# Grouped attention layers on one core: one product for the softmax denominators amid the next tile, reciprocals on transposed columns

## The reference

```python
N_HEADS, N_KV_HEADS, HEAD_DIM = 16, 4, 32
def rmsnorm(x, w, eps=1e-05):
    inv = jax.lax.rsqrt(jnp.mean(x * x, axis=-1, keepdims=True) + eps)
    return x * inv * w
q = (rmsnorm(x, norm_w) @ wq).reshape(B, T, 16, 32)
k = (cond @ wk).reshape(B, S, 4, 32)
v = (cond @ wv).reshape(B, S, 4, 32)
qg = q.reshape(B, T, 4, 4, 32)
scores = jnp.einsum('btgrd,bsgd->bgrts', qg, k) / sqrt(32)
attn = softmax(scores, axis=-1)
out = jnp.einsum('bgrts,bsgd->btgrd', attn, v).reshape(B, T, 512)
x = x + out @ wo
```

## Time and profile before

| | |
|---|---|
| median of 3 runs | 4080.01 us |
| the profiled run | 4083.46 us |
| its span, first to last instruction | 4081.7 us |
| TensorE busy | 3991.6 us (98%) |
| VectorE busy | 2434.2 us (60%) |
| ScalarE busy | 2094.2 us (51%) |
| GpSimd busy | 2035.3 us (50%) |
| granted clock of TensorE, mean | 0.989 |

### The profile page before, as it was taken

How to read it: one execution, slowest core, us unless ns; L and a number is a source line. 1 busy time by engine, 2 the same in 40 slices (tenths; PEclk the granted TensorE clock), 3 DMA queues, 4 the chain that set the end, 5 groups by cost and what they waited for, 6 DMA issues and landing times. The chain is left out here.

```text
span 4081.7 us, 52317 instructions
## 1 busy us (share of the span) xinstructions
PE 3991.6 (98%) x19446; PEld 2636.9 (65%) x19446; DVE 2434.2 (60%) x3455; ACT 2094.2 (51%) x2728; POOL 2035.3 (50%) x1097
## 2 busy tenths in 40 slices
PE   9999999998999999999968999999999999999999
PEld 7888888886566666666544555555555555555555
DVE  3221210011755566556638888888888888888885
ACT  3111221121544454444527776776677677767765
POOL 0000000001655566556736777677667677776766
PEclk9999999998999999999979999999999999999999
DMA  5343522233645555555423333333333333333332
GB/s 185 129 135 133 170 96 85 79 114 91 161 125 139 136 135 134 137 135 132 116 70 88 88 89 88 100 101 100 84 100 91 90 99 98 99 89 92 100 78 67
DMA packets 312792, 447.01 MB, mean 110 GB/s; under 512 B 44728, under 2 KB 116408, under 8 KB 312552
## 3 DMA queue, kind: packets, MB, share of 16 engines
q1 hardware_dynamic: 312552, 443.84, 38.8%
HBM read 215.07 MB, written 102.77 MB: 78 GB/s over the span
## 5 line engine op out<-in xcount | busy, mean ns | idle before, releaser
L1943 DVE TENSOR_REDUCE a_max_cols<-a_ps 128x1 f32<-128x512 f32 x1536 | 1028.5, 675 | 265.5 <-PE a_ps L2077 257.2
L1826 ACT ACTIVATE a_probs<-a_ps 128x1024 f32<-128x1024 f32 x768 | 774.6, 1024 | 378.3 <-PE a_ps L2108 372.7
L2077 PE MATMUL a_ps<-a_k_ops,a_q_ops 96*128 96x512 f32 x1536 | 653.3, 427 | 24.1 <-DVE a_max_cols L1943 17.5
L1724 POOL TENSOR_TENSOR a_sums<-a_probs 128x1024 f32<-128x1024 f32 x192 | 455.3, 2391 | 336.0 <-ACT a_probs L1826 336.0
L1047 DVE TENSOR_REDUCE a_max_cols<-a_ps 128x1 f32<-128x512 f32 x512 | 340.8, 688 | 273.4 <-PE a_ps L1211 273.3
L2077 PEld LDWEIGHTS a_ps<-a_k_ops,a_q_ops 96*128 96x128 f32 x1536 | 291.8, 190 | 312.5 <-issue 141.6
L2108 PE MATMUL a_ps<-a_q_ops,a_k_ops 128*128 128x512 f32 x1536 | 486.6, 398 | 1.1 <-ACT a_probs L1826 1.1
L807 POOL MEMSET a_ident<- 128x128 f32 x1 | 0.2, 204 | 975.5 <-issue 975.5
L1724 POOL TENSOR_TENSOR a_sums<-a_sums,a_probs 128x1024 f32<-128x1024 f32 x192 | 454.4, 2389 | 0.1
L2122 PE MATMUL a_ps<-a_probs,a_v 128*32 128x512 f32 x3072 | 411.1, 607 | 0.7 <-ACT a_probs L1826 0.6
L303 DVE TENSOR_TENSOR cp_c_lo<-cp_raw,cp_c_hi 128x1024 fp32r<-128x1024 f32 x64 | 78.4, 1226 | 529.2 <-ACT cp_c_hi L247 529.1
(11 more groups left out here) (154 smaller groups left out, 7347.0 us busy)
## 6 DMA issues: line engine op xcount, KB each, us to landing
a_k_ops<-k_scratch SPq DMA_DIRECT2D x192, 256.0 KB, 4.4
a_q_ops<-a_qn_hi SPq DMA_DIRECT2D x768, 64.0 KB, 2.0
k_scratch<-cp_out SPq DMA_DIRECT2D x88, 512.0 KB, 2.8
cp_raw<-in_ctx_t SPq DMA_DIRECT2D x64, 512.0 KB, 4.1
a_q_ops<-a_qn_hi SPq DMA_DIRECT2D x256, 128.0 KB, 2.3
x_raw<-out_t SPq DMA_DIRECT2D x25, 1024.0 KB, 7.2
a_q_ops<-a_qn_lo SPq DMA_DIRECT2D x384, 64.0 KB, 2.0
a_x_res<-out_t SPq DMA_DIRECT2D x92, 256.0 KB, 3.1
```

Source lines behind the costliest of these rows:

```text
L1724: pool.tensor_tensor(sums[:, hp], (probs if n < H else sums)[:, hp], probs[:, n], ALU.add)\
L1826: act.activation(probs[:, n], ps[:, 2 * (n % 2):2 * (n % 2) + 2, :], ACT.Exp).then_inc(exped, 1)
L1943: dve.tensor_reduce(max_cols[:, t % 2, col:col + 1], bank(b), AX.X, ALU.max, negate=True)\
L2077: pe.matmul(bank(b), q_ops[0:SHIFT, s, h, q * P:(q + 1) * P], k_ops[0:SHIFT, s, :], start=True, stop=True).then_inc(smax, 1)
```

## The change

GpSimd makes all six sums of probabilities of a tile: the four of before, then, once the tile's last outputs are done, sums 6 and 7, which are written over probabilities 6 and 7. The denominators become one group of products, moved behind outputs 0 of the next tile. VectorE transposes them out of PSUM in blocks of 32 x 32, so that each query's value stands in its own row and one column of each of 16 blocks is enough; it takes the reciprocal of these 16 columns, spreads them back with a second transpose whose input repeats the column, and makes the normalisation, which GpSimd made before. ScalarE no longer copies the denominators. The mean square goes the same way (transpose, 16 columns, transpose), its product moves to maximum 3 of tile 3 and to the bank of the outputs; the last quarter of squares is added ahead of sum 4 of tile 2, and one split of x moves from tile 3 to tile 0. The diff, cut to its core:

```diff
-            def sum_squares(n):
-                for k in range(1, CK):
+            def sum_squares(n, quarters=range(1, CK)):
+                for k in quarters:
...
-                if n >= H:
-                    pool.wait_ge(summed, g * SUMS + n - H + 1)
+                wait(pool, summed, g * SUMS + max(n - H + 1, 0))
                 pool.wait_ge(exped, g * NS + n + 1)
-                pool.tensor_tensor(sums[:, hp], (probs if n < H else sums)[:, hp], probs[:, n], ALU.add)\
-                    .then_inc(summed, 1)
+                if n >= NS - H // 2:
+                    pool.wait_ge(pv, (g + 1) * KT)
+                    pool.tensor_tensor(probs[:, n], sums[:, hp], probs[:, n], ALU.add).then_inc(summed, 1)
+                else:
+                    pool.tensor_tensor(sums[:, hp], (probs if n < H else sums)[:, hp], probs[:, n], ALU.add)\
+                        .then_inc(summed, 1)
...
-            def normalise(it, t):
-                g = tile_no(it, t)
-                pool.wait_ge(recip_done, (g + 1) * PARTS)
-                pool.wait_ge(out_taken, g + 1)
-                pool.tensor_tensor(stage[:, t % 2, :], out_raw[:, :], stage[:, t % 2, :], ALU.mult).then_inc(normed, 1)
...
+                    if there(it, t - 1):
+                        sum_probs(*at(it, t - 1), 6)
+                        sum_probs(*at(it, t - 1), 7)
...
+                    if t == 2 and there(it, 2 * T):
+                        sum_squares(it + 2, range(CK - 1, CK))
                     sum_probs(it, t, 4)
                     sum_probs(it, t, 5)
-                    if there(it, t - 1):
-                        normalise(*at(it, t - 1))
                     if t == 1 and there(it, 2 * T):
-                        sum_squares(it + 2)
+                        sum_squares(it + 2, range(1, CK - 1))
...
-            def take_denominators(it, t):
-                g = tile_no(it, t)
-                act.wait_ge(den_done, g + 1)
-                wait(act, o_lo, g - 1)
-                act.activation(stage[:, t % 2, :], bank(FB), ACT.Copy).then_inc(den_taken, 1)
...
-            def reciprocal(it, t, i):
+            def turn_denominators(it, t):
                 if there(it, t):
-                    n = S // PARTS
-                    if i == 0:
-                        dve.wait_ge(den_taken, tile_no(it, t) + 1)
-                    part = stage[:, t % 2, i * n:(i + 1) * n]
-                    dve.reciprocal(part, part).then_inc(recip_done, 1)
+                    g = tile_no(it, t)
+                    dve.wait_ge(den_done, g + 1)
+                    wait(dve, recip_made, g)
+                    dve.wait_ge(ms_step, 2 * inverted(*at(it, t + 1)))
+                    dve.transpose(turned_cols(), bank(FB)).then_inc(den_turned, 1)
+
+            def reciprocal(it, t):
+                if there(it, t):
+                    g = tile_no(it, t)
+                    dve.wait_ge(den_turned, g + 1)
+                    wait(dve, recip_done, g)
+                    dve.reciprocal(recip_col[:, :, :], cols[:, :, 0:1]).then_inc(recip_made, 1)
+
+            def spread_reciprocals(it, t):
+                if there(it, t):
+                    g = tile_no(it, t)
+                    dve.wait_ge(recip_made, g + 1)
+                    wait(dve, o_lo, g - 1)
+                    dve.transpose(stage[:, t % 2, :].rearrange("p (i j) -> p i j", j=d),
+                                  recip_col[:, :, :].broadcast_to([P, S // d, d])).then_inc(recip_done, 1)
+
+            def normalise(it, t):
+                if there(it, t):
+                    g = tile_no(it, t)
+                    dve.wait_ge(recip_done, g + 1)
+                    dve.wait_ge(out_taken, g + 1)
+                    dve.tensor_tensor(stage[:, t % 2, :], out_raw[:, :], stage[:, t % 2, :], ALU.mult)\
+                        .then_inc(normed, 1)
...
-                        invert_mean_square(it + 1, 2)
-                        invert_mean_square(it + 1, 3)
+                        split_x(it + 1, 1)
                     if t == 1 and there(it, T):
                         for k in range(0 if first else 2, CK):
                             split_x(it + 1, k)
                     if t == 3 and there(it, 2 * T):
                         split_x(it + 2, 0)
-                        split_x(it + 2, 1)
                     maximum(it, t, 1)
                     maximum(it, t, 2)
                     if t == 1:
                         where(dve, it, par, 1, lambda: rest_wo(it // B))
-                    reciprocal(*at(it, t - 1), 0)
                     maximum(it, t, 3)
+                    if t == T - 1 and there(it, 2 * T):
+                        turn_squares(it + 2, OUTB)
                     maximum(it, t, 4)
-                    reciprocal(*at(it, t - 1), 1)
+                    if t == T - 1 and there(it, 2 * T):
+                        invert_mean_square(it + 2)
+                    if t == 1 and first:
+                        spread_roots(1)
                     maximum(it, t, 5)
                     if there(it, t + AHEAD):
                         take_q(*at(it, t + AHEAD))
                     maximum(it, t, 6)
                     if t == 0 and first:
-                        mean_square(1, FB)
-                    if t == T - 1 and there(it, 2 * T):
-                        mean_square(it + 2, FB)
+                        turn_squares(1, FB)
+                    turn_denominators(*at(it, t - 1))
                     maximum(it, t, 7)
                     maximum(it, t, 8)
-                    reciprocal(*at(it, t - 1), 2)
+                    if t == 0 and first:
+                        invert_mean_square(1)
+                    reciprocal(*at(it, t - 1))
                     maximum(it, t, 9)
+                    spread_reciprocals(*at(it, t - 1))
                     maximum(it, t, 10)
                     if there(it, t - LAG):
                         add_result(it, t)
                     maximum(it, t, 11)
-                    reciprocal(*at(it, t - 1), 3)
-                    if t == 0 and first:
-                        for i in range(PARTS):
-                            invert_mean_square(1, i)
+                    normalise(*at(it, t - 1))
...
-                for h in range(H):
-                    pe.matmul(ps[h * d:(h + 1) * d, FB, :], ones[:, 0:d],
-                              probs[:, LATE * (H // 2) + h // 2, h % 2, :], start=True, stop=False,
-                              skip_group_check=True)
+                if there(it, t + 1 + AHEAD):
+                    pe.wait_ge(q_taken, g + 1 + AHEAD + 1)
                 pe.wait_ge(summed, (g + 1) * SUMS)
                 for h in range(H):
-                    last = pe.matmul(ps[h * d:(h + 1) * d, FB, :], ones[:, 0:d], sums[:, h // 2, h % 2, :],
-                                     start=False, stop=True, skip_group_check=True)
+                    last = pe.matmul(ps[h * d:(h + 1) * d, FB, :], ones[:, 0:d], probs[:, NS - H // 2 + h // 2, h % 2, :],
+                                     start=True, stop=True, skip_group_check=True)
...
-                    wait(pe, den_taken, tile_no(it, t))
-                    if there(it, t + AHEAD):
-                        pe.wait_ge(q_taken, tile_no(it, t) + AHEAD + 1)
-                    if t == T - 1 and there(it, 2 * T):
-                        pe.wait_ge(ms_step, MS * (it + 2) + 1)
+                    pe.wait_ge(den_turned, tile_no(it, t))
...
-                    denominators(*at(it, t - 1))
...
+                    if t == T - 1 and there(it, 2 * T):
+                        pe.wait_ge(out_taken, tile_no(it, t))
+                        sum_squares(it + 2, OUTB)
...
-                    if t == T - 1 and there(it, 2 * T):
-                        pe.wait_ge(q_taken, tile_no(it, t) + AHEAD + 1)
-                        sum_squares(it + 2, FB)
+                    denominators(*at(it, t - 1))
```

More of the change, by code:

```diff
@@ L1452, in grouped_layers @@
     scale = d ** -0.5
[L1453 to L1456 removed]
+    SUMS = (KT - 1) * (H // 2)
+    SQ = CK + 2
     LEAD = M + 6
@@ L1856, in batch @@
                         squares(1)
-                    if t == 1 and there(it, T):
-                        act.wait_ge(q_taken, (it + 1) * T)
+                    if t == (1 if it == 0 else 0) and there(it, T):
                         inv_rms(it + 1)
@@ L2023, in batch @@
                     maximum(it, t, 15)
-            mean_square(0, OUTB)
-            for i in range(PARTS):
-                invert_mean_square(0, i)
+            turn_squares(0, OUTB)
+            invert_mean_square(0)
             rest_wq(0)
+            spread_roots(0)
             for t in range(AHEAD):
@@ L2033, in _ @@
             pairs(dve, batch)
-            for i in range(PARTS):
-                reciprocal(N - 1, T - 1, i)
+            turn_denominators(N - 1, T - 1)
+            reciprocal(N - 1, T - 1)
+            spread_reciprocals(N - 1, T - 1)
+            normalise(N - 1, T - 1)
             add_result(N, 0)
```

63 lines of the change are left out of this document (37 added, 26 removed).

## The result

The changed kernel takes 4289.89 us (median of 4 runs, 4285.07 to 4294.19) against 4080.12: a ratio of 1.0514, 95% interval 1.0496 to 1.0532. It is 210 us slower, where 17 us faster was forecast, and far above the range. The profiled execution took 4285.07 us.

What follows compares the result with a forecast made beforehand. TensorE, busy 98% of the span, was taken as the bound. -82.6 (product) + 48 (GpSimd late) + 18 (weights) = -17 us: 4066 us for the profiled run, 4063 median; own range 4030 to 4085, whole range 4002 to 4112.

Steps and rivals of the forecast that it cites:

- TensorE is the bound and one product less is worth 0.86 us a tile: In each tile on TensorE, one product of denominators fewer saves 0.86 us, 82.6 us over 96 tiles.
- VectorE's new chain: VectorE's transpose of the denominators, taken as 0.69 us, ends 0.3 us before TensorE needs the bank: free.
- rival 3: VectorE's transposes are long (1.3 us) or the SBUF one takes turns with GpSimd: 4092 to 4107 us; chance 0.14.
- GpSimd's load: GpSimd's sums, remainders and squares need 71.7 us a block against TensorE's 77.0, 93%: throughput suffices.
- rival 4: GpSimd's sums arrive later than the denominators' product in every tile, so TensorE's path is not shortened: 4080 us; chance 0.03.
- The normalisation on VectorE: Asked amid sum 4, it ends 0.54 us after that sum; GpSimd's lateness then becomes TensorE's wait at maximum 14.
- How late GpSimd is: GpSimd's lateness makes TensorE wait 0.1, 0.75, 0.1 and 1.05 us in tiles 0 to 3: 48 us over 24 blocks.
- Rival 2: In tile 2 the normalisation waits 1.9 us for all of sum 4, clock may drop: 4080 to 4117 us; chance 0.22.
- Weights: At new weights (wo three times, wq twice) VectorE's remainders alternate with GpSimd's sums: 18 us, ends 0 and 30.
- Ends of the stage: The start saves about 4 us, the end waits about 4 us for sums 6 and 7: zero, plus or minus 5.

Runs made afterwards that it cites:

- both collisions away: Changed kernel with an SBUF transpose in place of the normalisation (multiplication left out) and tile 1's two x splits ahead of maximum 0: 4056.24 us, ratio 0.9937.
- three benches: Separate kernels computing nothing of the reference: VectorE asks amid trains of three GpSimd instructions, of ten, and of ten beside TensorE, ScalarE and loads; no total time given.
- the first bench: Computes nothing of the reference: 72 groups of three GpSimd additions, VectorE asking at growing delays with two-operand instructions or a 16-column scaling; no total time given.

## Why the prediction was wrong, step by step

- *TensorE is the bound and one product less is worth 0.86 us a tile*: nearly right in size (0.78 in the mean with both collisions away, 0.87 in the best tiles), as long as nobody is next. That ScalarE's copy of the denominators was worth nothing was wrong: without the rest of the change it is what is next (0.22 us a tile).
- *VectorE's new chain*: right. Transposes took 0.72 us out of PSUM and 0.70 out of SBUF, for the 0.69 that I took; the output projection did not wait. That excludes rival 3.
- *GpSimd's load*: right. The denominators waited 6.4 us for GpSimd, all of it at the end of the stage; rival 4 fell.
- *The normalisation on VectorE*: the step that failed. It read "whoever comes second waits for the whole instruction of the other" out of the earlier trace rows and priced every collision at the rest of one instruction, 0 to 2 us. That is a lower end. In the kernel three GpSimd instructions in a row went ahead of the normalisation, until GpSimd had nothing ready: 6.05 us where the rest of the sum was 1.98. The earlier trace rows show GpSimd giving way at 1183.5 with an instruction ready; they were 30 of 30, and I took a thing seen 30 times for a rule, though nearly all of the 30 asked at one place, 1.64 us into the sum. The range had no row for the other outcome.
- The Trainium skill, "SBUF — State Buffer", section "SBUF: two separate sides", says whoever starts first holds the port pair for its whole instruction. The trace agrees on the instruction that is running (every turn ends 0.55 us behind it). It does not follow that the blocked one is next, and the 6.05 us show that it need not be.
- *How late GpSimd is*: tile 2, where I saw the normalisation slip in ahead of sum 4, is the worst: it came 0.41 us after sum 4 had begun. Tile 1's splits did not hold sum 6 up; sum 6 held the second split, for 1.94 us of TensorE's time. Tile 3, which I had at 1.05 us, lost nothing there in most blocks (0.83 us; 3.16 to 4.85 in four).
- *Rival 2* named the place, tile 2, and the fall of the clock, which is 82 of the 98 us by which the other products grew. Its price was one turn, 1.9 us; 4.72 were paid. With the one wait before sum 5, which brings the price back to one turn, the time was 4146, so its 4080 to 4117 was too low even there: the splits' 1.94 us, which I had at 0.75, stay.
- *Weights*: forecast 18 us. In the kernel without the other collisions the five blocks take 7.7 us over the rest, where before they take 2.2 over 80.4: about 27, near the upper end of 30.
- *Ends of the stage*: 5.47 us of waiting at the end (4.98 without the collisions) against the 4 forecast; right in kind.

## What to carry to other kernels

An instruction with two SBUF operands that is moved to VectorE beside a GpSimd that works back to back must be priced from one turn up to GpSimd's next idle time, and GpSimd's ready queue at that moment is the row to read. A small scaling of one SBUF operand paid the same price here. One semaphore wait of GpSimd at the collision turns the long price into the short one (144 us here), and is cheaper to try than a new order, which only moves the collision. A gain on the bounding engine is paid out only if the runner-up, here ScalarE's copy or its queue behind a late GpSimd sum, is that much earlier too.

## What the runs showed of the hardware

- VectorE's blocked instruction can lose its turn to several GpSimd instructions in a row (6.05, 6.06, 7.17 and 8.18 us); in three benches it never did. What decides is open.
- A one-operand scaling of 16 columns from SBUF to SBUF took turns with GpSimd: 6.06 us in the kernel; in the first bench it ended 0.03 us behind the running addition. The same page and section of the Trainium skill counts a VectorE instruction in a two-port mode among those that take the pair; the turns fit that, but in which mode the scaling ran no run here shows. The transpose in 32 x 32 blocks out of SBUF (96 times, 0.70 us) and the reciprocal of 16 columns (0.23 us) took the same time whether GpSimd was running beside them or not.
- With the one wait before sum 5, 23 of 24 waits of TensorE of 1.35 to 1.50 us left the granted clock at 1.00 for the next four microseconds. In the changed kernel, of 19 waits of 1.94 to 1.97 us, 12 were followed by a clock of 0.50 within four microseconds and 7 were not; one of 4.72 was followed by a maximum of 0.80 us and a clock of 0.50 for about four. The wait of 2.60 us that the prediction read had a clock of 0.50 behind it; another of 2.60 in the same kernel, at 2239.79, left it at 1.00. So the length of one wait does not tell by itself what the clock does.
